# A decoder's mixture-of-experts stage: one list of 71 slots instead of two of 39, rows that carry tags, pads from ScalarE's queue, last sum on GpSimd

## The reference

```python
x = _rmsnorm(src + sa, norm1_w)                       # sa: attention, times Wo
shared = _swiglu(flat @ W_shared_in) @ W_shared_out
g_idx = jnp.argmax(g_probs, axis=-1)                  # 2 groups of 4 experts
p_expert = e_probs * g_prob
topv, topi = jax.lax.top_k(p_expert, TOPK)            # TOPK = 2 of E = 8
w = jnp.zeros((S, E)).at[jnp.arange(S)[:, None], topi].set(topv)
h = _swiglu(flat @ W1_shared)                         # 512 wide
for e in range(E):
    routed = routed + h @ W2_experts[e] * w[:, e:e + 1]
return _rmsnorm(x + shared + routed, norm2_w)         # the decoder then adds its own x
```

## Time and profile before

| | |
|---|---|
| time, median of 3 runs | 5806.1 us (5803.22 to 5812.38) |
| time of the profiled execution | 5799.72 us |
| its span, first to last instruction | 5797.9 us |
| mean granted TensorE clock | 0.954 |
| the stage's work | 5135 to 5798 us of the span |

### The profile page before, as it was taken

One profiled execution on the slowest core, in us unless ns is written; L12 is line 12 of the kernel. 1 busy time (PEld: TensorE's weight loads), 2 busy tenths in 40 slices (PEclk: granted clock), 3 DMA queues, 4 the chain that ended last, 5 costly groups with the idle time before them and its releaser, 6 DMA issues. The chain is left out here.

```text
span 5797.9 us, 139949 instructions
## 1 busy us (share of the span) xinstructions
PE 5047.6 (87%) x53862; PEld 3290.6 (57%) x53862; DVE 3899.8 (67%) x6898; ACT 3137.8 (54%) x4796; POOL 2453.7 (42%) x2096
## 2 busy tenths in 40 slices
PE   7788888888798799788889879997889999989994
PEld 3455555555576544477777768885532333346674
DVE  5999999999797855544444434444688888844424
ACT  5899999999655755322222223333435666642222
POOL 1788787888565533344444431113530000001214
PEclk9999999999999999799999999998789999999997
DMA  5202020110211233323333321112652222232256
GB/s 171 54 24 43 17 46 24 33 27 17 65 55 46 72 136 148 150 101 105 105 104 102 105 101 44 55 44 66 151 150 43 46 45 45 43 97 72 76 162 187
DMA packets 442677, 460.53 MB, mean 79 GB/s; under 512 B 228546, under 2 KB 377528, under 8 KB 433840
## 3 DMA queue, kind: packets, MB, share of 16 engines
q1 hardware_dynamic: 419984, 401.14, 24.5%
q0 software_dynamic: 8192, 25.17, 1.2%
q10 hardware_dynamic: 13856, 25.37, 1.2%
HBM read 278.15 MB, written 173.39 MB: 78 GB/s over the span
## 5 line engine op out<-in xcount | busy, mean ns | idle before, releaser
L539 POOL TENSOR_SCALAR attn_u<-attn_rel,attn_aux 128x1024 f32<-128x1024 f32 x512 | 1088.7, 2127 | 258.9 <-DVE attn_nm L568 248.1
L694 PE MATMUL attn_tp<-attn_ident,attn_pr 128*128 128x128 f32 x4096 | 571.1, 283 | 221.3 <-ACT attn_pt L630 219.2
L3426 DVE TENSOR_REDUCE attn_mx<-attn_mp 128x1 f32<-128x512 f32 x1024 | 652.6, 685 | 92.9 <-PE attn_mp L3505 91.9
L694 PEld LDWEIGHTS attn_tp<-attn_ident,attn_pr 128*128 128x128 f32 x4096 | 440.6, 142 | 457.9 <-ACT attn_pt L630 319.2
L560 DVE SCALAR_TENSOR_TENSOR attn_u<-attn_rel,attn_aux,attn_u 128x1024 f32<-128x1024 f32 x512 | 677.6, 1324 | 15.6 <-DVE attn_nm L568 7.3
L3490 ACT ACTIVATE attn_pt<-attn_st 128x1024 f32<-128x1024 f32 x512 | 506.5, 1022 | 284.5 <-PE attn_st L3516 284.0
L654 ACT ACTIVATE attn_pr<-attn_pr,attn_nm 128x1024 f32<-128x1024 f32 x512 | 622.4, 1216 | 51.1 <-DVE attn_nm L568 50.9
L568 DVE CUSTOM_DVE_ANT_0 attn_pr<-attn_u,attn_s 128x1024 f32<-128x1024 f32 x512 | 619.6, 1210 | 23.0 <-DVE attn_u L560 10.6
L630 ACT ACTIVATE attn_pt<-attn_tp 128x512 f32<-128x512 f32 x1024 | 585.7, 661 | 6.0 <-PE attn_tp L694 3.2
L3505 PE MATMUL attn_mp<-attn_kt,attn_qt 96*128 96x512 bf16 x1024 | 371.9, 394 | 18.3 <-DMA attn_qt<-s_q 17.5
L1686 PE MATMUL gin_pw<-gin_w,gin_xt 128*128 128x512 f32 x768 | 343.9, 601 | 3.2 <-ACT gin_qkv L1638 3.2
(11 more groups left out here) (542 smaller groups left out, 10728.1 us busy)
## 6 DMA issues: line engine op xcount, KB each, us to landing
s_qkv<-gin_qkv SPq DMA_DIRECT2D x32, 1536.0 KB, 5.0
core_qk<-s_qkv SPq DMA_DIRECT2D x32, 1024.0 KB, 5.1
attn_qt<-s_q SPq DMA_DIRECT2D x384, 64.0 KB, 3.0
attn_kt<-s_k SPq DMA_DIRECT2D x192, 128.0 KB, 4.6
moe_rows<-s_hid_s SPq DMA_DIRECT2D x78, 256.0 KB, 2.8
core_arow<-s_alr SPq DMA_DIRECT2D x32, 512.0 KB, 3.7
core_grow<-s_gar SPq DMA_DIRECT2D x32, 512.0 KB, 3.6
core_vv<-s_qkv SPq DMA_DIRECT2D x32, 512.0 KB, 3.5
```

The source lines that it names most:

```text
L539: pool.tensor_scalar(u[:, x % 4], rel[:, z % 2, 1], aux[:, s, 4 + NH + h:5 + NH + h], aux[:, s, 4 + 2 * NH + h:5 + 2 * NH + h], ALU.mult, ...
L694: ins = pe.transpose(tp[k][:, n], pr[:, x % BUF, (4 * k + n) * P:(4 * k + n + 1) * P], ident[:])
L3426: dve.reduce_max(mx[w % 2][:].rearrange("p h t a -> p (h t a)")[:, j:j + 1], bank(("row", number))[:], AX.X).then_inc(m["max_done"], 1)
```

## The change

It does seven things, all in `stage_moe`.

1. `HALF` becomes 16 pairs: there is one list of 2 x 32 + 7 = 71 slots, `tables` runs once, behind the last pair.
2. Each scattered row gets a tag of two numbers in a second scratch tensor, `tag_s`: where the result belongs (token + 4096 x choice) and the weight. So POOL issues eight indirect transfers for a pair, not four; SP loads 128 tags beside each slot's rows; `copy_out` multiplies by the weight, and POOL scatters each slot's results straight to their places in `y_t`. `gather` goes, and the third part reads `y_t` with plain loads from SP (`load_results`).
3. The pads are issued from ACT's queue, expert by expert, two ahead of the slots: `pad(0)`, `pad(1)`, then `pad(s + 2)` behind `copy_rows(s)`. `load_rows(s)` of the first eight slots waits for `pad_out[s]`.
4. `x5` is loaded during the slots, for all pairs (`x5_of`, partly into `wi`, which is free then).
5. The third part of all 16 pairs comes behind the last slot; its last sum moves from DVE to POOL (`last_sum`), and the output ring has four buffers.
6. PE does `prefix(i)` behind `inner(4i+3)` instead of ahead of it, and DVE `places(i)` behind `product(4i+3)`.
7. A fill of the rows past the last region (`overhang`) replaces one of 2 x 128 rows.

```diff
@@ SP
+            def overhang():
+                sp.wait_ge(m["tag_in"], 32)
+                sp.wait_ge(m["consts"], 1)
...
             def load_rows(s):
                 h = s // SL
                 if s % SL == 0:
                     for n in range(4):
                         sp.wait_ge(e["sc_out"][n], 32 * HT * (h + 1) // 4)
-                    sp.wait_ge(m["pad_out"], 16 * NE * (h + 1))
...
+                    for n in range(2):
+                        sp.wait_ge(e["tag_out"][n], 32 * HT * (h + 1) // 2)
+                    sp.wait_ge(m["table_done"], 1)
+                    sp.wait_ge(m["zero_out"], 32)
+                if s < NE:
+                    sp.wait_ge(e["pad_out"][s], 32)
                 need(sp, "tb_mm", s - 3)
...
                 sp.dma_start(rows[:, s % 4], d["hid_s"][bass.ds(row, P), :]).then_inc(e["row_in"][s % 4], 16)
+                need(sp, "y_copy", s - 3)
+                sp.dma_start(tags[:, s % 4], d["tag_s"][bass.ds(row, P), :]).then_inc(e["row_in"][s % 4], 16)
+
+            def load_results(c):
+                h = c // HALF
+                if c % HALF == 0:
+                    for n in range(3):
+                        sp.wait_ge(e["y_out"][n], 16 * ((LAST - n + 2) // 3))
+                need(sp, "acc2", c - 3)
+                for k in range(TOPK):
+                    at_ = k * T + c * 2 * P
+                    sp.dma_start(g[:, c % 4, k], d["y_t"][at_:at_ + 2 * P, :].rearrange("(z p) c -> p z c", p=P)).then_inc(e["g_in"][c % 4], 16)
@@ POOL
+                        pool.indirect_dma_start(d["tag_s"], bass.IndirectOffsetOnAxis(idx[:, t, k:k + 1], 0), tag[:, t, k], None
+                                                ).then_inc(e["tag_out"][t % 2], 16)
+
+            def results(s):
+                pool.wait_ge(m["home_done"], s + 1)
+                pool.wait_ge(m["y_copy"], s + 1)
+                pool.indirect_dma_start(d["y_t"], bass.IndirectOffsetOnAxis(home[:, s % 3], 0), yb[:, s % 3], None).then_inc(e["y_out"][s % 3], 16)
+
+            def last_sum(c):
+                pool.wait_ge(m["yn_done"], 2 * c + 2)
+                pool.tensor_tensor(y[:, c % 4], y[:, c % 4], x5_of(c), ALU.add).then_inc(m["out_done"], 1)
...
+            for s in range(LAST):
+                results(s)
+            pool.wait_ge(m["x5_in"], 16 * PAIRS)
+            for c in range(PAIRS):
+                last_root(c)
+                if c > 0:
+                    last_sum(c - 1)
+            last_sum(PAIRS - 1)
@@ DVE
             def copy_out(s):
-                dve.wait_ge(m["ob_mm"], s + 1)
+                dve.wait_ge(e["row_in"][s % 4], 32 * (s // 4) + 32)
                 if s >= 3:
                     dve.wait_ge(e["y_out"][s % 3], 16 * (s // 3))
-                dve.tensor_copy(yb[:, s % 3], ub[s % 2][:, 0:D]).then_inc(m["y_copy"], 1)
+                dve.tensor_copy(home[:, s % 3], tags[:, s % 4, 0:1]).then_inc(m["home_done"], 1)
+                dve.wait_ge(m["ob_mm"], s + 1)
+                dve.tensor_scalar(yb[:, s % 3], ub[s % 2][:, 0:D], tags[:, s % 4, 1:2], None, ALU.mult).then_inc(m["y_copy"], 1)
...
+                dve.wait_ge(e["g_in"][c % 4], 32 * (c // 4) + 32)
+                both = acc[:, 2 * c:2 * c + 2]
+                dve.tensor_tensor(both, both, g[:, c % 4, 0], ALU.add).then_inc(m["acc1"], 1)
+                dve.wait_ge(m["acc1"], c + 1)
+                dve.tensor_tensor(both, both, g[:, c % 4, 1], ALU.add).then_inc(m["acc2"], 1)
...
                     product(4 * i + 2)
+                    product(4 * i + 3)
                     places(i)
-                    product(4 * i + 3)
@@ ACT
+            def pad(n):
+                if n == 0:
+                    act.wait_ge(m["table_done"], 1)
+                row = act.value_load(pads[0:1, 0, n:n + 1], min_val=0, max_val=SORTED - P)
+                act.dma_start(d["hid_s"][bass.ds(row, P), :], zero[:]).then_inc(e["pad_out"][n], 16)
+                act.dma_start(d["tag_s"][bass.ds(row, P), :], spare[:, 0, n]).then_inc(e["pad_out"][n], 16)
...
+            for n in range(2):
+                pad(n)
             for s in range(LAST):
                 copy_rows(s)
...
+                if s + 2 < NE:
+                    pad(s + 2)
+            for c in range(PAIRS):
                 last_squares(c)
-                if c > HALF:
+                if c > 0:
                     store(c - 1)
             store(PAIRS - 1)
@@ PE
                 if i is not None:
                     inner(4 * i + 1)
                     inner(4 * i + 2)
+                    inner(4 * i + 3)
                     prefix(i)
-                    inner(4 * i + 3)
```

More of the change, by code:

```diff
@@ L3611, in stage_moe @@
         pick, posn, posf = r.sb("pick", [P, 2, TOPK, NE]), r.sb("posn", [P, 2, NE]), r.sb("posf", [P, TILES, TOPK])
-        fe, shift, moved = r.sb("fe", [P, NE]), r.sb("shift", [P, HT * TOPK, NE]), r.sb("moved", [P, HT * TOPK])
-        idx, gidx = [r.sb(n, [P, TILES, TOPK], mybir.dt.uint32) for n in ("idx", "gidx")]
-        wsel = r.sb("wsel", [P, TILES, TOPK])
+        idx = r.sb("idx", [P, TILES, TOPK], mybir.dt.uint32)
+        tag, spare, tags = r.sb("tag", [P, TILES, TOPK, 2]), r.sb("spare", [P, 2, NE + 7, 2]), r.sb("tags", [P, 4, 2])
+        home = r.sb("home", [P, 3, 1], mybir.dt.uint32)
         cnt, num, cumi = r.sb("cnt", [P, NE]), r.sb("num", [P, NE]), r.sb("cumi", [P, NE])
@@ L3666, in load_pair @@
                     sp.dma_start(src[:, p % 2, z], d["src1"][(p * 2 + z) * P:(p * 2 + z + 1) * P, :]).then_inc(e["a_in"][p % 2], 16)
[L3668 to L3672, removed]
+            def overhang():
+                sp.wait_ge(m["tag_in"], 32)
+                sp.wait_ge(m["consts"], 1)
+                sp.dma_start(d["hid_s"][ZERO_ROWS:ZERO_ROWS + 7 * P, :].rearrange("(n p) c -> p n c", p=P),
+                             zero[:].rearrange("p (o c) -> p o c", o=1).to_broadcast([P, 7, HID])).then_inc(m["zero_out"], 16)
+                sp.dma_start(d["tag_s"][ZERO_ROWS:ZERO_ROWS + 7 * P, :].rearrange("(n p) c -> p n c", p=P), spare[:, 0, NE:]).then_inc(m["zero_out"], 16)
             def load_rows(s):
@@ L3721, in _ @@
                     load_pair(nxt + 1)
-                if i == HALF + 1:
-                    pad(0)
+                if i == 5:
+                    overhang()
             for s in range(3):
@@ L3726, in _ @@
             for s in range(LAST):
-                if s == 2:
-                    pad(1)
                 if s + 3 < LAST:
                     load_rows(s + 3)
[L3731 to L3735, removed]
-            for c in range(HALF, PAIRS):
-                load_x5(c)
-            for n in range(2):
-                sp.wait_ge(e["out"][n], 16 * PAIRS // 2)
+                if s >= NE and s % 4 == 0:
+                    load_x5(s // 4 - 2)
+            for c in range(PAIRS):
+                load_results(c)
+            for n in range(4):
+                sp.wait_ge(e["out"][n], 16 * PAIRS // 4)
         @block.gpsimd
```

133 lines of the change are left out of this document (40 added, 93 removed).

## The result

The changed kernel takes 5785.42 us (median of 20 runs, 5775.26 to 5795.89), the kernel before in the same rounds 5805.57 (20 runs, 5796.31 to 5814.86): ratio 0.9971, interval 0.9965 to 0.9977. It is faster, by 20 us by the medians and by 17 (0.29%) by the ratio, instead of 37; the time lies inside the range but 16 us above the forecast.

A forecast was written before the change was run, and what follows sets the result against it. TensorE was taken to set the pace up to the last slot, the chain of token work behind it. A -40.9, B +17.4, C -30.2 and D +16.5 sum to -37.2, from 5806.1 to 5769 us; range 5748 to 5793 (8 in 10).

The forecast's parts named there:

- A: Last stage, first load to last product of counts: sixteen TensorE waits (-25.7) and nine clock drops (-15.2) go, -40.9 us.
- D: Behind the last slot's copy out: third part of all sixteen pairs, from 63.6 to 80.1 us, +16.5.
- B: Last product of counts to slot 8's transposes: scatters, pads and first loads, from 30.4 to 47.8 us, +17.4.
- C: Slot 8's transposes to the end of the last copy out: 63 slots instead of 70, 168.6 to 138.4 us, -30.2.
- The rival in which the clock keeps falling: Pairs: the wait goes but the clock drops remain, A = -25.7, time 5784 us; chance 0.2.
- a new wait: Pairs: pos_done late for the logits or POOL late for the root, half of A lost, about 5790 us; chance 0.07.
- the last is issued at 8.1 and lands 2.7 later: In B: last of POOL's eight scatters, us counted from the last product of counts, landed at 10.8.
- tags landed 2.8: In B: slot 0's tags land 2.8 us after issue, as the rows do, putting slot 0 at 14.8 us.
- the three rings: In B, slots 2 to 7: copy, pad, load, transposes two slots on; 9.4 us each, 28.2 together.
- 63 x 2.167 + 1.9 = 138.4: In C: 63 slots at 2.167 us each, plus 1.9 for the last slot's way through the engines.
- Tags gate the slots: Slots: 8-byte tags landing over 3.7 us after the copy slow each slot, up to 5834 us; chance 0.08.
- The ring: In D: squares, variance, root, POOL's addition, ScalarE's store issue, then the next squares: 4.1 us a pair.

The follow-up runs named there:

- tags_64: Changed kernel with tags of 64 bytes instead of 8, and three buffers instead of four for results read back: 5767.0 us, 0.9934 of the kernel before.
- order_only: Kernel before with only the two moved calls (prefix behind inner(4i+3), places behind product(4i+3)): 5755.3 us, ratio 0.9912.
- order_pads_act: Kernel before with the two moved calls and the second list's pads on ScalarE's queue, one each third slot from slot 4: 5754.1 us, ratio 0.9899.

## Why the prediction was right on A and D and wrong on B and C

- **A, -46.5 for -40.9.** The mechanism and both its terms held: sixteen waits gone, nine drops gone with them, nothing late behind them. Two small terms were missing. The pairs came 21.07 us apart, 0.32 less than 22.95 - 1.56: without the break in them the products of `inner` take 0.26 less and those of `prefix` 0.1, 5 us in sixteen pairs. And the count for the first list's table, 1.2 us in the middle of this part, is gone. For the time this was luck: it made up for 5.6 of the 24.4 us that B and C cost more than forecast. The rival in which the clock keeps falling, 0.2, did not occur; neither did a new wait.
- **B, +32.4 for +17.4.** The step that failed is "the last is issued at 8.1 and lands 2.7 later" with "tags landed 2.8" and "landing 2.1". All three were prices of pieces of 2 KB in the earlier trace rows, put on pieces of 8 bytes. The last scatter took 8.7: +6.0, just what slot 0 was late (20.8 for 14.8). In the three rings the pad's landing took 3.0 to 3.4 instead of 2.1 and the tags' 4.7 to 5.2 instead of 2.8, together +9.8; from the transposes to the issue of the pad's tags it took 1.2 instead of 2.15, -2.8; so the rings were 11.7, 11.4 and 12.5 long instead of 9.4, +7.4. Slot 8 followed slot 6 by 6.4 instead of 4.8, +1.6: slot 6's eight products took 3.28 us where those of slot 7 took 1.73. With the 6.0 that makes the 15. tags_64, with 1.7 to 3.0 for the same landings, gave 46.1 for my 47.8; its slot 0 came at 14.8 as forecast, its first ring took 7.7. The row from which I should have read was the one that I kept for the rival, 3.4 for a load in 8-byte pieces, and even that was low.
- **C, -20.8 for -30.2.** The step that failed is "63 x 2.167 + 1.9 = 138.4": the slots took 2.310 us on average. The reasons given for it ("DVE's added copy of one column lies in its idle time" and what follows) have no term for the queue that rows, tags and residual loads share, sixteen of these among the slots where eight had been. C stayed at 146.4 to 153.2 in every run with the narrow tags or the sixteen loads in place, and was 139.9 and 140.5 in the two without both. Which of two crowded things delays which inside the queues, and why the stalls stand behind every other load, is not settled.
- **The slower rival.** "Tags gate the slots" asked for a landing over 3.7 us in every slot. That occurs in B, not in the steady slots, where TensorE waited 3.4 us in all. (The chances put below 5794.5 add up to 0.885, not to 0.87.)
- **D, +19.2 for +16.5.** The ring held, 4.06 for 4.1, in part because misses cancel: the root took 1.05 us where the sum had 0.82, the addition 1.31 for 1.4, and there was less between them than the 0.3. The Trainium skill's "SBUF — State Buffer", section "SBUF: two separate sides", says that a GpSimd instruction and a DVE one with two SBUF inputs exclude each other. The trace agrees: 1.49 for 0.47 beside the addition, 1.05 beside DVE's additions for the root, which takes 0.70 without one. But the time that the forecast had worked out under this rule, 1.64 for the addition, did not come: the price lay on DVE, outside the ring, and 0.3 of it on the root. I had put down 3.1 us a pair for DVE without GpSimd; it was 2.91. The 2.6 us by which D is over the sum stand at its end: "the 5.5 from the last sum to the end" was 9.8, since GpSimd's drain, 7.9 us here, comes behind a last sum on GpSimd.
- **The kernel before.** The stage differences by the profiled executions are smaller than those of the medians (-15.7 and -20, order_only -41 and -51). The profiled execution of the kernel before, 5799.7 us, lay 6 us under its median, those of the changed kernel and of order_only 7 and 9 us above theirs; whether the stage or the ones ahead made that difference is not told by one trace each.

## What to carry to other kernels

Cost a transfer by a row with pieces of the same size, not of the same queue; where there is none, take the dearer end for the forecast and not for the rival. When a change has several parts, run each alone: here one reorder of two calls held all the gain, and hid that the larger rewrite lost 30 us of it until a few small things were put right. Before an engine gets work "because it is idle", look whether that work stands in the loop of waits that sets the pace: the addition on the idle GpSimd made a ring of 4.06 us a pair, the same addition on the busier DVE one of 2.91.

## What the hardware showed beyond the forecast

- **Scatters of 8-byte pieces end long after their bytes have moved.** The DMA slices from 5496 to 5517 us in the changed kernel, 0.53 us each (busy share in tenths, then GB/s): the last bytes move before 5510, and the last scatter counts as landed at 5514.1.

```profile
DMA  0001910039000480005993391000000000000019
GB/s 0 0 0 55 374 70 2 0 117 374 8 2 0 179 320 0 2 0 207 386 363 47 129 351 21 0 0 0 0 0 0 0 0 0 0 0 0 0 35 203
```

  With 64 bytes a piece the pads' tags landed in 1.7 to 2.1 us in tags_64 (five whose landing the trace has); with 8 bytes in 3.0 to 7.8, median 4.3 (eight, in the changed kernel). The Trainium skill's "DMA: Bandwidth & Descriptors", section "Latency and other measured facts", gives a transfer's fixed cost as about 2 us, with HBM as the slowest target; the wide pieces agree with it, the narrow ones do not.
- **A hole under a wrong name.** In order_only and in both runs of order_pads_act, not in the kernel before, one step between two slots, that to slot 46, took 8.4 to 8.6 us. The timeline of order_only there:

```profile
5608.14 0.42 DVE L3934 COPY moe_yb<-moe_ub 128x256 f32<-128x256 f32 x1 [6.53 <-DMA core_grow<-s_gar]
5609.57 1.09 ACT L4035 ACTIVATE moe_rt<-moe_ua 128x512 f32<-128x512 f32 x2 [6.56 <-DMA core_vv<-s_qkv]
5610.31 3.78 PE L4170 MATMUL moe_ub<-moe_w,moe_rt 128*128 x8 [4.39 <-ACT moe_rt L4035]
```

  DVE and ScalarE stand still together for 6.5 us, put down to loads of a stage long past. The semaphores on which the two lines wait say more: they are `ob_mm` and `tb_mm`, which TensorE's products raise. In these slots a raise mostly stands in the trace 0.3 to 0.4 us behind the start of its product; here it stands 5.2 us (at 5608.1) and 6.1 us (at 5609.6) behind products that the trace has at 5602.9 and 5603.5. So both engines waited for TensorE, whose products were reported done late. Why is open. The hole is the 6 us by which order_only's C exceeds that of the kernel before.
